# Mask of the dense heads moved from VectorE to ScalarE and TensorE, in pieces of 512 tokens

## What is computed

```python
q = (x @ Wq_pk).reshape(b, n, 2, HEADS, 32).transpose(2, 0, 1, 3, 4)
sim = einsum('pbnhd,pkhd->pbnhk', q, pk_keys)        # two sides of 64 scores
scores, idx = top_k(sim, 16)
score = scores[0][..., :, None] + scores[1][..., None, :]   # 16 x 16 pair sums
final_scores, pk_idx = top_k(score, 16)
final_scores = softmax(final_scores)                 # weights of 16 table rows
...
```

## Time and profile before

| | |
|---|---|
| time, median of 3 runs | 15191.99 us (15181.57 to 15207.99) |
| time of the profiled execution | 15184.2 us |
| its span | 15182.0 us |
| stretch with the dense pieces | 5902 to 14940 us: 9038 us |
| granted clock, whole span / dense stretch | 0.713 / 0.72 |

### The profile page before, as it was taken

One profiled execution on the slowest core, in us unless ns is written; L12 is line 12 of the kernel. 1 busy time (PEld: TensorE's weight loads), 2 busy tenths in 40 slices (PEclk: granted clock), 3 DMA queues, 4 the chain that ended last, 5 costly groups with the idle time before them and its releaser, 6 DMA issues.

```text
span 15182.0 us, 143792 instructions
## 1 busy us (share of the span) xinstructions
PE 9984.7 (66%) x39356; PEld 5998.2 (40%) x39356; DVE 10276.2 (68%) x24001; ACT 5847.3 (39%) x13853; POOL 7907.9 (52%) x6892
## 2 busy tenths in 40 slices
PE   1564555555456643777777777777777777777777
PEld 1351222122131222445445445445445445444444
DVE  3334888888838657776676676676676676676662
ACT  0113333333310122454454454444444444444453
POOL 3000677676500003766666666666666666666662
PEclk9555777777757765677777777677677777677776
DMA  1000223222200001111111111111111111111110
GB/s 23 0 14 9 98 110 109 96 109 98 89 10 11 9 4 39 49 46 50 45 46 50 46 45 49 45 45 49 46 45 49 46 46 50 46 45 49 46 47 21
DMA packets 305126, 731.80 MB, mean 48 GB/s; under 512 B 130243, under 2 KB 170738, under 8 KB 269915
## 3 DMA queue, kind: packets, MB, share of 16 engines
q0 software_dynamic: 201216, 405.72, 10.3%
q1 hardware_dynamic: 103178, 317.81, 6.2%
HBM read 706.25 MB, written 8.42 MB: 47 GB/s over the span
## 4 chain that ended last, share of the span: by engine, by line
PE 34%; DVE 10%; ACT 10%; DVEq 4%; issue 3%; ACTq 0%
PE l3m_S L2286 8%; PE l3m_acc L2327 7%; PE l3m_O L2303 5%; PE l3m_DX L2316 4%; ACT l3m_spread L2416 4%; PE l3m_T L2293 4%; DVE l3m_W L2666 2%; ACT l3m_E L2455 2%; DVEq L2657 2%; PE l3m_DX L2314 1%; PE l3m_T L2252 1%; PE l3m_T L2273 1%; DVE l3m_side L2604 1%; ACT l3m_probT L2451 1%; DVEq L2574 1%
## 5 line engine op out<-in xcount | busy, mean ns | idle before, releaser
L2234 POOL DMA_INDIRECT l3m_got<-in_l_table,l3m_row x6144 | 5956.8, 970 | 3152.8 <-issue 1837.0
L2327 PE MATMUL l3m_acc<-l3m_W,l3m_values 128*128 128x256 f32 x4096 | 1869.3, 549 | 1678.2 <-DVE l3m_W L2666 1426.3
L2666 DVE SCALAR_TENSOR_TENSOR l3m_W<-l3m_DX,l3m_E 128x256 f32<-128x256 f32 x2048 | 863.2, 422 | 2133.5 <-ACT l3m_E L2455 2057.1
L2416 ACT ACTIVATE l3m_spread<-l3m_got,l3m_weight 128x128 f32<-128x128 f32 x6144 | 2082.6, 488 | 0.0
L2327 PEld LDWEIGHTS l3m_acc<-l3m_W,l3m_values 128*128 128x128 f32 x4096 | 837.2, 255 | 2022.6 <-DVE l3m_W L2666 1587.0
L2455 ACT ACTIVATE l3m_E<-l3m_DX 128x256 f32<-128x256 f32 x2048 | 787.0, 384 | 1946.9 <-PE l3m_DX L2316 1944.8
L2451 ACT ACTIVATE l3m_probT<-l3m_T 128x512 f32<-128x512 f32 (+3 forms) x1280 | 682.4, 533 | 1985.2 <-PE l3m_T L2293 1983.1
L1262 POOL TENSOR_TENSOR m_mul<-m_st,m_wide_c 128x2048 f32<-128x2048 f32 x256 | 1157.3, 4521 | 150.0 <-DVE m_st L1415 143.8
L2303 PE MATMUL l3m_O<-l3m_vo_g,l3m_probT 128*128 128x64 f32 x6528 | 978.6, 294 | 178.0 <-ACT l3m_probT L2451 178.0
L2303 PEld LDWEIGHTS l3m_O<-l3m_vo_g,l3m_probT 128*128 128x128 f32 x6528 | 895.5, 210 | 297.3 <-ACT l3m_probT L2451 251.5
L1295 PE MATMUL m_W<-m_mul,tower_ident 128*128 128x512 f32 (+1 forms) x1536 | 839.9, 669 | 207.3 <-POOL m_mul L1262 206.3
(11 more groups left out here) (673 smaller groups left out, 18827.3 us busy)
## 6 DMA issues: line engine op xcount, KB each, us to landing
m_wide_c<-l1a_c SPq DMA_DIRECT2D x256, 1024.0 KB, 4.7
l3m_got<-in_l_table,l3m_row POOLq DMA_INDIRECT x6144
l3m_values<-in_l_table SPq DMA_DIRECT2D x32, 512.0 KB, 4.5
l0i_img<-in_l_x SPq DMA_DIRECT2D x4, 1024.0 KB, 8.0
l2r_x<-l2a_hT SPq DMA_DIRECT2D x8, 512.0 KB, 5.4
qp_inw<-in_q_inw SPq DMA_DIRECT2D x1, 2336.0 KB, 8.0
l_kept<-l0t_xt,l0t_row POOLq DMA_INDIRECT x128, 2.2
l1a_c<-m_mul SPq DMA_DIRECT2D x16, 128.0 KB, 2.6
```

The source lines that it names most:

```text
L2234: pool.indirect_dma_start(got[:, unit % GOT, j, :], None, table, bass.IndirectOffsetOnAxis(ap=row[:, unit // QUAD % RING, unit % QUAD, j:j ...
L2327: pe.matmul(acc[:, 0:HALFQ], values[:, tile, :], W[:, k % 2, :], start=(tile == 0), stop=(tile == TILES - 1)).then_inc(blended, 1)
L2416: last = act.activation(spread[:, unit % 2, :, j], got[:, unit % GOT, j, :], ACT.Copy, scale=weight[:, g % RING, t, j:j + 1])
L2666: dve.scalar_tensor_tensor(W[:, k % 2, :], DX[:, 0:HALFQ], ABSENT, E[:, k % 2, :], ALU.is_gt, ALU.mult).then_inc(masked, 1)
```

## The change

Pieces become 512 tokens wide, so a row has 32 pieces and a step two. VectorE no longer takes part in a piece. Piece k now goes like this: `level(k)` on TensorE puts the sums of ranks of 512 tokens into the whole bank `DX`; `lift(k)` on ScalarE computes V = relu(100 - sum) in bf16, which is 0 for a picked row (sum over 99) and at least 1 otherwise; `cross(k)` on TensorE overwrites `DX` with the three parts of the exponent and adds `push x V`, where `push` is -256 on the diagonal, so that a row not picked has an exponent of -256 or lower; `grow(k)` on ScalarE takes the exponential straight into `W`, and `blend(k)` multiplies. `store` replaces two `store_half`.

```diff
-HALFQ = QUAD * P // 2
+APART = 256.0
...
+            dve.tensor_scalar(push[:], ident[:], -APART, None, ALU.mult)
+            dve.memset(least[:], ABSENT + 1.0)
...
-        return [64 * r + 4 * q + i for i in range(4)] if 0 <= r < ROWS else []
+        return [TILES * r + 2 * q + i for i in range(2)] if 0 <= r < ROWS else []
...
+            def level(k):
+                if k % TILES == 0:
+                    pe.wait_ge(taild, k // TILES + 1)
+                if k:
+                    pe.wait_ge(grown, k)
+                pe.matmul(DX[:], sel[:, k % TILES, :], ranksT[:, k // TILES % 2, :],
+                          start=True, stop=True).then_inc(levelled, 1)
+
             def cross(k):
...
+                pe.wait_ge(lifted, k + 1)
                 for i, x in enumerate((high, mid, tail)):
...
+                    pe.matmul(DX[:], sel[:, k % TILES, :], x[:, k // TILES % 2, :], start=(i == 0), stop=False)
+                pe.matmul(DX[:], push[:], V[:], start=False, stop=True).then_inc(crossed, 1)
...
-                pe.wait_ge(masked, k + 1)
...
+                pe.wait_ge(grown, k + 1)
+                pe.matmul(acc[:], values[:, tile, :], W[:], start=(tile == 0),
+                          stop=(tile == TILES - 1)).then_inc(blended, 1)
...
+            def onward(k):
                 if k >= 1:
                     blend(k - 1)
-                cross(k)
+                level(k)
...
+                    for c in range(max(3, depth[n] // 4 + 1)):
+                        if c <= depth[n] // 4:
+                            flip(n, c)
+                        if todo and c == 0:
+                            cross(todo[0])
+                        if todo and c == 1:
+                            onward(todo[1])
+                        if todo and c == 2:
+                            cross(todo[1])
+                        if c <= depth[n] // 4:
+                            mixing(n, c)
...
+            def lift(k):
+                act.wait_ge(levelled, k + 1)
+                act.activation(V[:], DX[:], ACT.Relu, bias=least[:], scale=-1.0).then_inc(lifted, 1)
+
             def grow(k):
                 act.wait_ge(crossed, k + 1)
-                act.activation(E[:, k % 2, :], DX[:, HALFQ:], ACT.Exp).then_inc(grown, 1)
+                act.activation(W[:], DX[:], ACT.Exp).then_inc(grown, 1)
...
-            def admit(k):
-                dve.wait_ge(grown, k + 1)
-                if k >= 2:
-                    dve.wait_ge(blended, k - 1)
-                dve.scalar_tensor_tensor(W[:, k % 2, :], DX[:, 0:HALFQ], ABSENT, E[:, k % 2, :],
-                                         ALU.is_gt, ALU.mult).then_inc(masked, 1)
```

More of the change, by code:

```diff
@@ L2000, in l3_ffn, with fold_keys @@
             sel, counts = s.sb("sel", [P, TILES, P], BF16), s.sb("counts", [P, 2, TOPK], BF16)
-            fold_keys(nc, A, ident, wsim, iota, wq, wo, mask, lanes, sel, counts)
-            mix_heads(nc, A["l3_table"], h, hT, ident, ones, wsim, iota, wq, wo, mask, lanes, sel, counts)
-def fold_keys(nc, A, ident, wsim, iota, wq_all, wo_all, mask, lanes, sel, counts):
+            push, least = s.sb("push", [P, P], BF16), s.sb("least", [P, 1])
+            fold_keys(nc, A, ident, wsim, iota, wq, wo, mask, lanes, sel, counts, push, least)
+            mix_heads(nc, A["l3_table"], h, hT, ident, ones, wsim, iota, wq, wo, mask, lanes, sel, counts, push,
+                      least)
+def fold_keys(nc, A, ident, wsim, iota, wq_all, wo_all, mask, lanes, sel, counts, push, least):
     with Scope(nc, "l3w") as w:
@@ L2084, in attended, with mix_heads @@
     return kind, g
-def mix_heads(nc, table, h, hT, ident, ones, wsim, iota, wq, wo, mask, lanes, sel, counts):
+def mix_heads(nc, table, h, hT, ident, ones, wsim, iota, wq, wo, mask, lanes, sel, counts, push, least):
     wsim_h = wsim[:].rearrange("d (p h k) -> d h p k", p=2, h=HEADS)
@@ L2180, in mix_heads @@
         diag, invT = u.sb("diag", [P, QUAD, P]), u.sb("invT", [P, 2, CH])
-        E, W, stage = u.sb("E", [P, 2, HALFQ]), u.sb("W", [P, 2, HALFQ]), u.sb("stage", [KV, CH])
+        V, W, stage = u.sb("V", [P, CH], BF16), u.sb("W", [P, CH]), u.sb("stage", [KV, CH])
         S, T = u.ps("S", [P, SEQ]), u.ps("T", [P, CH])
@@ L2198, in mix_heads @@
         PER_B = 12 * ROWS // B
-        HEAD_PIECES = QUAD * 2 * TILES
+        HEAD_PIECES = QUAD * TILES
         def arrived(unit):
@@ L2356, in _ @@
                 if todo:
-                    piece(todo.pop(0))
-                    piece(todo.pop(0))
+                    onward(todo[0])
                 elif r == ROWS and q == 0:
-                    blend(64 * ROWS - 1)
+                    blend(TILES * ROWS - 1)
                 made = made_at(r, q)
@@ L2366, in _ @@
                     pe.wait_ge(expd, n + 1)
-                    for c in range(depth[n] // 4 + 1):
-                        flip(n, c)
-                        if todo:
-                            piece(todo.pop(0))
-                        mixing(n, c)
-                for k in todo:
-                    piece(k)
+                    for c in range(max(3, depth[n] // 4 + 1)):
[9 more added lines that the diff above has]
+                            mixing(n, c)
+                elif todo:
+                    cross(todo[0])
+                    onward(todo[1])
+                    cross(todo[1])
                 if made is not None:
@@ L2487, in _ @@
                 unit = unit_at(r, q, 1)
-                if todo:
-                    grow(todo.pop(0))
-                part_up(unit, 0)
                 if n is not None:
@@ L2493, in _ @@
                 if todo:
-                    grow(todo.pop(0))
-                part_up(unit, 1)
-                if n is not None:
-                    for c in range(depth[n] // 4 + 1):
+                    lift(todo[0])
+                part_up(unit, 0)
+                for c in range(max(3, depth[n] // 4 + 1) if n is not None else 3):
+                    if n is not None and c <= depth[n] // 4:
                         take_flip(n, c)
-                        if todo:
-                            grow(todo.pop(0))
-                for k in todo:
-                    grow(k)
-                part_up(unit, 2)
+                    if todo and c == 0:
+                        grow(todo[0])
+                        part_up(unit, 1)
+                    if todo and c == 1:
+                        lift(todo[1])
+                        part_up(unit, 2)
+                    if todo and c == 2:
+                        grow(todo[1])
                 made = made_at(r, q)
```

46 lines of the change are left out of this document (12 added, 34 removed).

## The result

The changed kernel takes 14019.36 us, the median of 4 runs (14010.32 to 14026.52), against 15190.17 us (15181.57 to 15207.99) for the kernel before beside it. The ratio is 0.9227 (95% interval 0.9213 to 0.924): 7.7% less. The forecast was 14320 us; it had the sign right and was 301 us too high. The time lies where the rival "GpSimd becomes the bound" had put it, 13900 to 14050.

The account below looks back on a forecast made before the run. The prediction took TensorE's work plus hand-overs to VectorE's late queue as the bound. From 15184, -1675 +209 +614 -270 +150 +100 gave 14312, or 14320 us against the median of the runs; range 13960 to 14980.

Parts of the forecast that it names:

- GpSimd becomes the bound: Rival, chance 0.10: with a clock well over 0.75 GpSimd's gathers set the pace; 13900 to 14050 us.
- The floor of the gathers: GpSimd's gathers and their gaps cannot be shed, so at most 1272 us can be won: 13912 us.
- GpSimd close behind, +100: Dense stretch: GpSimd's buffers even out shallow and deep quarters not quite fully; +100 us.
- the clock's, -270: TensorE in the dense stretch: longer runs between waits raise its granted clock from 0.72 to 0.75; -270 us.
- the predicted 209: TensorE's work: one more stream of 512 columns per 512 tokens, less the fixed cost of 1024 fewer blends; +209 us.
- VectorE's waits, -1675: TensorE before `blend`: all its waiting for VectorE's `W` and `stage` goes; -1675 us.
- Bare hand-overs to ScalarE through V and W: TensorE waits for `lift` and `grow` where other work does not cover them; 0.84 us a step, part of +614.
- spreads ahead of the flips: ScalarE's spread shares stand ahead of `take_flip`, which the mixing needs; 0.36 us a step, part of +614.
- VectorE as the limit in rank steps: Rank steps: TensorE and VectorE queues of nearly equal length lose 1.2 us a step handing over; +150 us.
- the first rival: Lateness moves to the exponential behind VectorE's row maximum, half of 1675 us stays; 14550 to 15130 us, chance 0.16.
- the flips' wait: TensorE's flips before chunk 0 wait for ScalarE's `prob`: some 150 us expected, 800 if the lateness moved.
- The third rival: TensorE waits bare for ScalarE in `cross` and `blend`, 0.95 us per hand-over, 1946 us; slower, 15914 us; chance 0.09.

## Why the prediction was right and wrong

**The bound before was read rightly.** VectorE's mask was late and not slow: `blend` waited 1674.8 us for VectorE before and not at all after. The kernel before without gathers still takes 15250 us, so GpSimd was no part of it as far as two chips can be compared.

**The floor of the gathers was worked out rightly and given too small a chance (0.10).** The condition that the prediction named for it, a clock well over 0.75, came true with 0.81. It had 13912 us. Measured are 14017.65 in the profiled execution, 106 more: the gathers take 982 ns in the mean instead of 970 (+80), their gaps 1868.7 instead of 1837.0 (+32), 27.7 us of waits are left, and the part behind the last start is 244.3 us (14017.65 - 13773.4) instead of 277.4 (-33). The 80 us are all in long gathers: 530 of them take over 1 us, together 233 us more than the median, where the trace of the kernel before has 539 with 154 us. The term "GpSimd close behind, +100" is some 444 us by the kernels with and without gathers, on two chips.

**The term that was most wrong is the clock's, -270.** The direction was right, the size was not. TensorE had 6789.5 us of work, and with the predicted 209 more it would be 6998.5 at the old clock; it is busy for 6174.5. So 824 us came from the clock, 0.72 to 0.81, beyond even my bound of 679 us at 0.80. This rests on the 209, and the trace can check it. Split by the level granted at each moment, TensorE was busy for 4043 us at the low and 2747 at the high one before, and for 2448 and 3727 after. If the same work takes twice as long at the low level, the work grew by 260 us at the old mix of levels and the clock gave 875; with the factor 1.9 of `blend` in the earlier trace rows (1.01 to 0.53 us) it is 196 and 811. Without gathers the same sum gives 6824 + 209 - 5938 = 1095, or some 990 with the missing records filled in. With 554 us more from here the sum would have fallen to 13758, below the floor and below the range, and the rival would have been the forecast. The time still lies in the range because GpSimd's floor held it up; that is in part luck. That the longer runs between waits lifted the clock is what the rows suggest, not what they show: the 512-wide streams came with the same change. No single number of the views puts the kernels in order. Idle shares of 25, 22 and 20% have 0.72, 0.81 and 0.83 (before, after, after without gathers), but the kernel with the early crossing also has 20% and only 0.77.

**VectorE's waits, -1675, were right; of what replaced them the sum was near, but not the places.** In the dense stretch TensorE's idle time fell from 2249 to 7878 - 6174.5 = 1703.5, by 545 us, where my terms had 1675 - 614 - 150 - 100 = 811. With the clock's 554 and these 266 the sum becomes 14312 - 554 + 266 = 14024, and 14017.65 were measured. Bare hand-overs to ScalarE through V and W cost 175.0 + 138.4 = 313 us; I had 0.84 us a step for them, 430. I had another 184 for spreads ahead of the flips. The mixing does wait 188 us more, but that is a coincidence: without gathers, with the spreads in the same places, it waits 101.6 us, less than the 239.2 of the kernel before without gathers. With gathers ScalarE's spreads, which stand ahead of `take_flip`, wait 432.5 us for their data, and the mixing's longest wait grows from 0.7 to 10.3 us. So the extra wait goes with late data, and the spreads' places as such cost nothing that shows. The sentence that the prediction fails if V and W pass 1200 us stayed far from true. But the scores' wait for the exponential grew from 70 to 682 us, where "VectorE as the limit in rank steps" had +150. I had treated the scores as cover behind `level`, when by the code `scores(n+1)` itself waits for `expd` of tile n, the tile of the flips behind it. The lateness moved after all, to a third of its size: the first rival was half right in mechanism, and its price of half of 1675, 837, is 225 more than the 612 that came. The sign that I had named for it (the flips' wait) could not have shown it, since the scores stand ahead of the flips. One reading against this rival was wrong as well: without masks VectorE has not 8 us of work in a step outside the rank steps but 11.5, 10.9 and 8.1 in the three quarters (52.59, 50.30 and 39.18 in the earlier trace rows, less 16 masks of 0.422, by 4).

**Why it cost so little time.** Taking the mask off VectorE and changing the order pull in opposite directions. The order alone, one piece less ahead of the scores, is +855 us. With it and without the masks the scores wait 732 us instead of 1776.

**ScalarE.** `lift` is 683 ns and `grow` 594, for which I had 0.68 and 0.60. The Trainium skill, "ScalarE: Activation LUTs", section "What ACT_TABLE_LOAD costs", puts an activation with a pointer bias at 280 ns + 0.833 ns an element, an estimate of 706 ns for 512; this case's trace has 683. The rule of its section "Rules for kernel authors" is to use VectorE for relu. No run here has the relu on VectorE, so the rule itself is untested; with the mask moved to ScalarE, among other edits, the kernel is 7.7% faster. The third rival, bare hand-overs, would have needed 0.6 us each; measured are 313 / 2048 = 0.15 us of TensorE's waiting for V and W.

**TensorE's work, +209.** Of its parts the timeline shows the streams of 512 columns 0.42 to 0.43 us apart at the low clock and 0.21 to 0.22 at the high one, as assumed; the sum is bracketed by the 196 to 260 us above. No run isolates it.

## What to carry to other kernels

When a short operation is late because it stands behind long work in its engine's queue, moving it to an engine with room can pay; here ScalarE was no slower at it either (683 ns against two masks of 422). But look at what then stands ahead of the next reader: a moved wait must be priced at every instruction that waits for the same engine, not only at the one that named it. Work out the floor of each engine that runs behind (first to last start, less its waits) before giving chances: when a forecast comes within a few per cent of such a floor, one term of the wrong size makes the floor the answer. And carry TensorE's granted clock as a term with wide bounds; here it gave more than any wait but the first.

## What the runs showed of the hardware

*The gathers' pace.* An indirect DMA of 128 rows takes GpSimd 0.944 us (median) and the next starts 0.30 us later, 1.25 us apart, in the result's profile as in the one below. Some take up to 1.998 us. Of the result's 6144 gathers 854 overlap in time with a VectorE operation (TENSOR_TENSOR) that writes `l3m_hot`, and 356 of these take over 1 us; of the other 5290 only 174 do. That the one slows the other is not shown by any run.

*Late hand-overs on some chips.* In the kernel before with the changed order and all gathers TensorE ends its crossing at 13458.70, but ScalarE, idle, starts the exponential that waits for it only at 13473.48 (its timeline, all engines):

```profile
13458.15 0.94 POOL L2234 DMA_INDIRECT l3m_got<-in_l_table,l3m_row  x1 [0.30 <-issue]
13458.28 0.42 PE L2316 MATMUL l3m_DX<-l3m_tail,l3k_sel 128*128 128x256 bf16 x1
...
13459.40 0.94 POOL L2234 DMA_INDIRECT l3m_got<-in_l_table,l3m_row  x1 [0.30 <-issue]
...
13473.48 0.38 ACT L2456 ACTIVATE l3m_E<-l3m_DX 128x256 f32<-128x256 f32 x1 [18.91 <-remote]
```

GpSimd goes on gathering at its usual pace meanwhile. In the dense stretch TensorE, ScalarE and VectorE are all idle for over 1.5 us at once in 499 places (2588 us) of that profile. The changed kernel, the same program on two chips, has 17 such places (58 us) in the result's profile and 567 (2303 us) at 18504 us; on that second chip it has 6 (14 us) without gathers. With all gathers the kernel before takes 19.9 to 20.1 ms on these chips, with a quarter less 18.1 to 18.3, without them 15.25; the gathers themselves are not slower (0.94 us). So the hand-overs come late there only with the gathers. A gather costs the kernel before 1.14 to 1.20 us of time when a quarter of them is left out, and (20107 - 15251) / 6080 = 0.80 us in the mean over all that were. What in them does so, and why on these chips and not on that of the result, stays open; no run tells it.
